# A fused attention and quantised feed-forward block: small statistics moved to GpSimd, two of four finals split between ScalarE and GpSimd, opening and step order rewritten

## The reference

```
x = x + tanh(g_x) * cross_attention(x, ctx)      # (32, 256, 256)
x = x + tanh(g_f) * ffn(layernorm(x))
ffn: h = layernorm(x)*g1 + b1'   ; h = bitlinear(h, w1, b1)   # 256 -> 1024
     h = gelu(h)
     h = layernorm(h)*g2 + b2'   ; h = bitlinear(h, w2, b2)   # 1024 -> 256
bitlinear(x, w, b): rows of x rounded to 8 bits by 127 / max|x|,
                    w rounded to -1, 0, 1 by 1 / mean|w|, product scaled back
```

## Time and profile before

| | |
|---|---|
| median of 3 runs (lowest, highest) | 402.39 us (400.57, 402.53) |
| the profiled execution | 400.17 us |
| its span, first to last instruction | 398.4 us |
| VectorE busy, share of the span | 330.2 us, 83% |
| TensorE matmuls | 304.1 us, 76% |
| ScalarE | 277.9 us, 70% |
| GpSimd | 220.9 us, 55% |
| granted TensorE clock, mean | 0.949 |

### The profile page before, as it was taken

The page is one execution under the profiler, slowest core; times in us unless marked ns, Lnnn a source line. Parts: engine busy times, 40 slices in busy tenths (PEclk is TensorE's granted clock), DMA queues, the critical chain, the costliest instruction groups (busy, mean ns, idle before and its releaser), DMA issues. The chain is left out here.

```text
span 398.4 us, 5821 instructions
## 1 busy us (share of the span) xinstructions
PE 304.1 (76%) x1690; PEld 187.9 (47%) x1690; DVE 330.2 (83%) x794; ACT 277.9 (70%) x446; POOL 220.9 (55%) x118
## 2 busy tenths in 40 slices
PE   2887295868888888888888888888888766758364
PEld 2776153434646464646464646464646342414043
DVE  0389366888999999999999999999999995957782
ACT  1314447678697979797979797979797968678431
POOL 4021444829484848484848484848485858454600
PEclk9999689989999999999999999999999996969669
DMA  7665404119183828383838383838270707062635
GB/s 226 244 225 181 132 0 130 56 53 185 54 186 107 190 102 182 108 183 110 184 107 184 108 183 109 180 111 172 67 170 18 170 17 160 26 115 71 135 77 160
DMA packets 97686, 51.56 MB, mean 129 GB/s; under 512 B 86535, under 2 KB 88768, under 8 KB 97654
## 3 DMA queue, kind: packets, MB, share of 16 engines
q1 hardware_dynamic: 96758, 51.14, 50.7%
q10 hardware_dynamic: 896, 0.04, 0.1%
HBM read 21.78 MB, written 8.41 MB: 76 GB/s over the span
## 5 line engine op out<-in xcount | busy, mean ns | idle before, releaser
L337 POOL TENSOR_TENSOR y<-u,g_bc 128x1024 f32<-128x1024 f32 x64 | 150.3, 2368 | 62.5 <-DVE parts L594 49.7
L694 DVE TENSOR_TENSOR y<-y,slot_c 128x1024 f32<-128x1024 f32 x64 | 77.7, 1214 | 9.9 <-PE slot_c L965 9.8
L698 DVE TENSOR_REDUCE amax<-y 128x1 f32<-128x1024 f32 x64 | 78.1, 1220 | 2.2
L432 ACT ACTIVATE q<-y,s 128x1024 f16<-128x1024 f32 x64 | 69.8, 1139 | 11.5 <-DVE s L725 11.5
L459 ACT ACTIVATE junk<-u,usum 128x1024 bf16<-128x1024 f32 x64 | 73.5, 1149 | 2.1
L1003 PE MATMUL bank_f<-w2T,q2T 128*128 128x256 f16 x512 | 66.1, 276 | 2.6 <-DVE res L745 2.4
L320 POOL TENSOR_TENSOR rstd<-var,half_neg 128x8 f32<-128x8 f32 x18 | 29.5, 1641 | 69.0 <-DVE var L645 56.6
L965 PE MATMUL slot_c<-ln_rows,rows 128*128 128x512 bf16 x128 | 41.3, 406 | 30.8 <-DVE y L694 16.3
L944 PE MATMUL bank_q<-wvo,ctxT 128*128 128x256 f32 x232 | 59.7, 387 | 0.0
L1003 PEld LDWEIGHTS bank_f<-w2T,q2T 128*128 128x128 f16 x512 | 50.2, 99 | 14.6 <-DVE res L745 4.8
L423 ACT ACTIVATE q<-h,s 128x256 f16<-128x256 f32 x64 | 27.3, 496 | 32.7 <-DVE s L685 32.7
(11 more groups left out here) (114 smaller groups left out, 426.8 us busy)
## 6 DMA issues: line engine op xcount, KB each, us to landing
c_in<-in_ctx SPq DMA_DIRECT2D x16, 512.0 KB, 3.4
x_in<-in_x SPq DMA_DIRECT2D x16, 512.0 KB, 4.1
out<-res SPq DMA_DIRECT2D x32, 256.0 KB, 2.8
y<-in_L_ffn_w SPq DMA_DIRECT2D x2, 1024.0 KB, 9.3
u<-in_L_xattn_Wkv SPq DMA_DIRECT2D x1, 1024.0 KB, 6.8
u<-in_L_xattn_Wout SPq DMA_DIRECT2D x1, 1024.0 KB, 10.0
q2T<-q SPq DMA_TRANSPOSE x64, 3.3
g_bc<-in_L_ffn_ln_g SPq DMA_DIRECT2D x1, 512.0 KB, 4.5
```

The lines of the kernel that those rows point to most:

```text
L337: nc.gpsimd.tensor_tensor(y[:, k % 2, t, :], u[:, t, :], g2_bc[:, :], ALU.mult).then_inc(gain2_done, 1)
L432: nc.scalar.activation(q2[:, t, :], y[:, k % 2, t, :], ACT.Copy, scale=s2[:, t:t + 1]).then_inc(q2_done, 1)
L694: nc.vector.tensor_tensor(line, line, slot_c[:, :], ALU.add).then_inc(y_done, 1)
L698: nc.vector.tensor_reduce(amax2[:, t:t + 1], y[:, k % 2, t, :], AX.X, ALU.max, apply_absolute_value=True).then_inc(amax2_done, 1)
```

## The change

It has three parts.

*Statistics.* `deviations`, `split` and `variance` go from VectorE to GpSimd. `join` becomes four `bn_aggr` on VectorE and `norm_first`, two small operations, on GpSimd. The two scale chains `first` and `second` become one, `scales`, over both kinds at once.

*Finals.* Tiles 0 and 1 of every group but the last are copied by ScalarE out of bank_f, scaled by d2 (`evict`, body i for group i-2), and GpSimd adds the residual one body later (`add_residual`). Tiles 2 and 3 stay with VectorE; their second product moves to body i for group i-3. Tiles of the last group stay as they were.

*Order and buffers.* y has three buffers, `rows` two; attention from group 3 on is written to slot_a. On ScalarE q2 of tiles 2 and 3 stands behind the squares, ahead of the next q1. On SP the loads, transposes and stores stand in a new order. In the opening, Wv and Wout arrive in halves, x ahead of w1; VectorE copies the second half of wvT; w1 is rounded and turned after the first residuals, and w2 in body 0 through slot_c, copied by VectorE.

```diff
+                def add_residual(k):
+                    wait(pool, evicted, k + 1)
+                    wait(pool, stored[k % 2], 32 * (k // 2))
+                    nc.gpsimd.tensor_tensor(res[:, k % 2, 0:2, :], scaled[:, :, :],
+                                            x1[:, k % SETS, 0:2, :], ALU.add).then_inc(added, 1)
...
+                def split(n):
+                    shape = [P, T, KINDS, NPART]
+                    if n == 0:
+                        wait(pool, std_done, min(i + 2, S + 2))
+                        wait(pool, var1_done, min(i + 2, S))
+                        wait(pool, var2_done, min(i, S))
+                        wait(pool, scales_ready, scales_after(i - 1))
+                        wait(pool, rows_done, i + 1)
...
                 if -1 <= i <= S:
-                    wait(pool, split_steps, split_count(i))
+                    deviations()
+                if -1 <= i <= S + 1:
+                    for n in range(5):
+                        split(n)
...
                 if live(i - 1):
-                    if i > 1:
-                        gain(i - 1, 2)
                     gain(i - 1, 3)
+                if 0 <= i - 3 < S - 1:
+                    add_residual(i - 3)
                 if live(i + 1) and i > -1:
                     gain_first(i + 1)
+                if live(i + 2) and i > 0:
+                    norm_first(i + 2)
                 if live(i):
                     gain(i, 0)
                     gain(i, 1)
+                    gain(i, 2)
...
+                if live(i):
+                    variance(i)
                 if -1 <= i + 1 <= S:
                     root(i + 1)
...
+                def evict(k):
+                    wait(act, ffn_done, T * k + 2)
+                    wait(act, added, k)
+                    for t in range(2):
+                        op = nc.scalar.activation(scaled[:, t, :], bank_f[:, D * t:D * (t + 1)],
+                                                  ACT.Copy, scale=d12[:, (k + 1) % 2, 1, t:t + 1])
+                    op.then_inc(evicted, 1)
...
             for i in bodies:
+                if live(i - 3):
+                    turn_second(i - 3, 2)
+                    turn_second(i - 3, 3)
                 if live(i):
                     turn_first(i)
-                if live(i - 2):
-                    for t in range(T):
-                        turn_second(i - 2, t)
+                if live(i + 4) and i + 4 > 1:
+                    load_x(i + 4)
+                if live(i + 5) and i + 5 > 2:
+                    load_context(i + 5)
                 if live(i - 3):
                     store(i - 3, 0)
+                if live(i - 2):
+                    turn_second(i - 2, 0)
+                    turn_second(i - 2, 1)
+                if live(i - 3):
                     store(i - 3, 1)
```

More of the change, by code:

```diff
@@ new lines, in split @@
+                def split(n):
[6 more added lines that the diff above has]
+                        wait(pool, rows_done, i + 1)
+                    else:
+                        wait(pool, split_steps, split_count(i - 1) + n)
+                    if n % 2 == 0:
+                        value = (stat_t, rest[:, :, :], rest[:, :, :])[n // 2]
+                        op = nc.gpsimd.tensor_copy(
+                            parts_q[:, :, :, 3 * (n // 2):3 * (n // 2) + 3],
+                            value.unsqueeze(3).to_broadcast(shape))
+                    else:
+                        value = (stat_t, rest[:, :, :])[n // 2]
+                        op = nc.gpsimd.tensor_tensor(rest[:, :, :], value,
+                                                     parts_q[:, :, :, 3 * (n // 2)], ALU.subtract)
+                    op.then_inc(split_steps, 1)
@@ L486, in body @@
                     quantise(i - 2, 1)
-                if 0 < i <= S:
-                    take_rows()
+                if live(i + 3) and i > 0:
+                    take_context(i + 3, 1)
+                if live(i):
+                    for t in range(T):
+                        gelu(t)
+                        square(t)
+                if 0 <= i - 2 < S - 1:
+                    evict(i - 2)
                 if live(i - 2):
@@ L836, in body @@
                     if i == S:
-                        for n in range(4):
-                            second(i - 1, n, slice(0, 2))
+                        scales(slice(1, 2), slice(0, 2))
                     row(i - 1, 2)
                     row_max(i - 1, 2)
+                if live(i - 3):
+                    final(i - 3, 2)
+                    final(i - 3, 3)
                 if live(i - 1):
@@ L984, in hidden @@
                         wait(pe, rows_copied, i + 2)
+                    if t == 0 and i > 0:
+                        wait(pe, x1_done, 2 * min(i + 3, S))
                     wait(pe, gelu_done, T * i + t - 1)
@@ L1054, in body @@
                     correction(i - 1, 0)
-                if live(i + 3) and i > -3:
-                    turn_context(i + 3, 0)
+                if live(i + 3):
+                    turn_context(i + 3, 1)
+                if live(i - 3):
+                    second_product(i - 3, 2)
+                if live(i - 1):
+                    correction(i - 1, 1)
                 if live(i):
@@ L1080, in body @@
                     attention(i + 3, 0)
+                    attention(i + 3, 1)
             for i in bodies:
```

652 lines of the change are left out of this document (293 added, 359 removed).

## The result

The changed kernel takes 410.16 us (median of 4 runs, 409.33 to 411.04); beside it the kernel before took 402.31 (400.57 to 402.53). The ratio is 1.0205, 95% interval 1.0165 to 1.0246: 2% slower, where 3% faster was forecast. The profiled execution of the changed kernel is 409.39 us, its span 407.6 against 398.4.

What follows compares the result with a forecast made beforehand. VectorE was taken to pace steps at 19.98 us; after the change, loops through several engines would. Steps -8.9, opening -5.8 and end +3.6 gave -11.1 us, execution 389.1, scaled to 391.2 us; range 380.5 to 402.0.

Steps and rivals of the forecast that it cites:

- A: Opening, up to the first gelu of step 1: forecast 5.8 us shorter than the 73.91 before.
- step 1's gelu near 68.1: End of the opening: attention and first gelu earlier, w2's preparation in between; 68.1 instead of 73.91, bounds 0 and -7.8.
- B: The 14 step periods between the first gelus of steps 1 and 15: 274.6 us against 283.5, -8.9.
- loop 2: Steady step through GpSimd's statistics, TensorE and gelu: 18.35 us at full clock, hidden under loop 1 by 0.7.
- loop 1: Steady step through ScalarE's copies and quantisations, the q1 transpose and four gelu and square pairs: 19.05 us with hops.
- The low-level loop: loop 2 with TensorE at the 1.2 GHz level: 19.75 us, expected in about three steps of four.
- a gap of 3.2 us: TensorE's idle time before the next rows are turned, expected to let its granted clock fall.
- C: From the first gelu of step 15 to the end: +3.6 us on 41.0, bounds +1 and +6.
- SP store of group 14 ahead of the last q2 transposes: End, SP's queue: a store waiting for GpSimd's addition delays the last four q2 transposes; the new wait behind +3.6 us.
- The clock holds: Rival: TensorE's gap does not lower the clock, loop 1 alone paces, 14 periods 266.7 us, time 383; chance 0.25.
- GpSimd becomes the bound: Rival: GpSimd's splits and hops cost 0.5 us or more each, steps take 21.6 us, time 423; chance 0.13.
- 402.0 as upper end: Slow end of the forecast range: q1's transpose delayed by a train of transposes, or 0.8 us more on GpSimd.

Runs made afterwards that it cites:

- e1: The changed kernel with GpSimd's first multiplication of step 0 waiting until VectorE's six scale operations are done: 403.75 us, ratio 1.0057.
- e2: The changed kernel with all four q2 transposes of step 15 ahead of both stores of step 14 on SP: 408.77 us, ratio 1.0175.
- e11: e8 plus eight identity transposes behind each of step 15's first three corrections and 34 ahead of the first turn of w2: 386.90 us, ratio 0.9644.
- e8: e7 with finals of tiles 0 and 1 back on VectorE, shorter fillers and SP's order alone at the end: 388.35 us, ratio 0.9656.
- e12: e6 plus transposes of the identity ahead of the turn of rows in steps 13 to 17: 400.34 us, no ratio given.
- e7: The changed kernel with the edits of e1, e3 and e6 and identity transposes in steps 13 to 17: 391.60 us, ratio 0.9721.
- e6: e2 plus ScalarE quantising q2 of tiles 2 and 3 of step 14 ahead of the scaled copies: 407.65 us, ratio 1.0132.
- e3: The changed kernel with TensorE repeating each step's first four context transposes three more times, ahead of the turn of rows: 401.30 us, ratio 0.9995.
- e9: As e3, but with the four context transposes repeated once instead of three times: 401.86 us, ratio 1.0016.

## Why the prediction was wrong

**A, the failed step: "step 1's gelu near 68.1".** The sum costed VectorE's chain by durations alone and looked for no GpSimd work beside it. Three of six scale operations were each held for a whole multiplication: 4.3 us net by e1, counted from step 0's first gelu. The rows that could have shown it are in the kernel before, where a scale operation at 56.34 takes 2.12 us and ends at 58.46, with a multiplication that ends at 58.43:

```profile
56.08 2.35 POOL L337 TENSOR_TENSOR y<-u,g_bc 128x1024 f32<-128x1024 f32 x1 [0.21 <-ACT u L451]
56.34 2.12 DVE L681 TENSOR_SCALAR stat<-amax_inv,deq_inv 128x4 f32<-128x4 f32 x1
```

I had read the steady stage, where GpSimd waits for VectorE's splits and the two rarely meet. The Trainium skill, SBUF — State Buffer, "SBUF: two separate sides", states the rule: VectorE and GpSimd share a port pair under an exclusive lock, which VectorE needs for an operation with two SBUF inputs or in a 2-port mode; whichever starts first holds it for the whole instruction, and the other is blocked fully. The trace agrees for the two-input operations (0.17 us becomes 2.2); that the one-input operation that was held ran in a 2-port mode is not shown by a run here.

The rest of the 10.4: the first gelu came at 47.67, not 44.4, which is 3.3. The forecast had q1 at 36 and w1T copied at 41; q1 was quantised from 39.77 on, and TensorE turned w1 only at 42.40, straight behind an attention, so that its copies were done at 45.4. The first attention started 1.5 us earlier than before (21.86), not 3, but that is not the cause by itself: in e2 it starts at 20.47 and the first gelu at 47.97. Turns of w2 ran at the low level, 1.0 us by e11. Some 1.8 us between the two gelus stay unexplained.

**B, the clock falls as described, but the loops are too short.** At the high level the pieces up to the product (3.19 against 3.25) and GpSimd's splits (0.29 and 0.27 against 0.25 to 0.35) were right; these casts and subtractions take 1.3 times VectorE's 0.22 and 0.20, not twice. The first product's last wait is for the q1 transpose, as forecast:

```profile
236.10 0.10 PEld L984 LDWEIGHTS slot_a<-b_rows,rows 128*128 128x128 bf16 x1 [0.33 <-DMA q1T<-q]
```

But loop 2 does not hide 0.7 us under loop 1. It was put at 18.35 and is 19.2: 4.6 from the last square to the turn of rows, 3.2, 1.5, and 9.96 for the four pairs (237.61 to 247.57) where I had 9.5. Both loops tie, and with loop 1 shortened (e8) the period stays. That 19.24 lies near the forecast's 19.05 is luck in part: the longer pairs made up for a shorter way to q1's landing (7.8 us from the last square, against 7.9 and 0.15 of hops).

The low-level loop was put at 4.1 + 4.65 + 1.5 + 9.5 = 19.75; measured it is 4.4 + 4.4 + 1.97 + 9.5 = 20.3. Product to gelu also stretches, from 1.51 to 1.97 us, which I had left at its high-level value, and GpSimd's chain was 0.3 over. 11 of the 14 periods are 19.85 us or longer, with a mean of 20.4; the mean of all 14 is 20.1 where I had 19.6, and that is the 7 us. The share of steps that fall, three of four, came out (seven of ten), but by luck: it rested on a gap of 3.2 us, longer than the 2.52 ahead of 84.50. Attention ends later than I had it, the gap is 1.3 to 1.6, nearer to the 1.17 at which the kernel before kept its level, and the forecast had no estimate for a gap between the two.

**C, the named wait is not the bound.** "SP store of group 14 ahead of the last q2 transposes" is in the trace, yet e2, with it removed, is no shorter there. Scales were complete at +28.9, as forecast (+28.5), and the addition for step 14 at +32.0 (+31.6). Step 14's other store then waits for finals that start at 396.91, behind two second products at 1.9 us, and holds the last transposes in turn. What lengthens the rest is second products at the low level in a chain with the finals, about 4 us by e12 and e7 against e6; the two orders are worth 1 at most.

**The rivals.** "The clock holds" did not happen, but e3 shows that it was the right lever: its 14 periods are 273.7 us. With nearly all steps at the high level (e8) they are 269.7, not the 266.7 that this rival had, by the same longer loop. "GpSimd becomes the bound" through slow small operations is excluded by the rows: no split takes over 0.3 us, although GpSimd's chain is in the loop that paces. The range left out that one GpSimd instruction could block VectorE at all; 402.0 as upper end was too near. A side slower than before was held possible at 0.13, for another reason than the one that came.

## What to carry to other kernels

Where GpSimd gets more of the work, look in the trace for VectorE operations that are longer than elsewhere and end with a GpSimd instruction, and order the two so that a short chain never starts beside a long multiplication: here one wait more gave 6.4 us by the medians, 4.3 of them traced to the opening. Taking load off the pacing engine makes another one idle; if that is TensorE, read its idle times and the granted clock of the next stretches, and price every piece up to the next engine at the low level. Here a few repeated transposes in the gap were worth 7 us, where the change without them cost 8.

## What the runs showed of the hardware that was not expected

- Which VectorE operations are held. With a multiplication running (2.36 us), two-operand operations of 8 columns went from 0.13 or 0.17 to 2.2, a one-operand scalar operation in fp32 of 8 columns from 0.17 to 2.33, and one of 2048 columns from 1.28 to 2.26. The reciprocal at 53.74 ran in 0.20 beside the third multiplication. In the other direction GpSimd's operations of 4 columns went from 0.19 to 1.10 and 1.17 beside VectorE's roundings.
- A shift of 0.2 us between two engines decides whether VectorE is held two or three times, 2.2 us of the total. Two variants of one kernel can differ by 0.5% in that way with none of it due to their edit; comparing pieces of the profile, not only times, shows it. Each variant has one profile, so whether the shift goes with the build or with the execution is open.
- Idle times of 0.90 us did not bring the granted clock down, six of nine of 1.33 to 1.61 did; the other three (1.34, 1.60 and 1.34) were followed by products of 1.04 us all the same, and so was one of 1.76 in e9 (turn of rows at 114.38). What makes the difference is not shown.
- In the profiled execution of e12 the clock stood at 0.95 throughout the steady stage, as in the row below, did not fall although TensorE idled 1.01 to 1.03 us ahead of most turns of rows and 1.92 ahead of one, and eight products took 1.06 us. The periods were 19.4 and the execution 394.18 us against 400.3 to 402.1 in its other three. What sets this value is open; it was seen once.

```profile
204.00:206.00 2.00, 2.00 (x12) 1.55 (x11) 1.38 (x6) 2.00 (x6) 1.46 (x3) 0.95 0.00 0
206.00:208.00 2.00, 1.70 (x11) 1.23 (x9) 1.48 (x4) 2.00 (x5) 1.68 (x5) 0.95 0.40 79
```
